# Edge sums by bucket on one core: two of each 16 batches scattered row by row instead of one, and TensorE's first loop placed at the head of a fetch block

## What is computed

```python
edge_aggr = zeros((6250, 128)).at[row].add(edge_features)      # 206,250 rows of 128 fp32
combined  = concat([x, edge_aggr, global], -1) @ W_c + b_c
h   = softplus(combined @ W1 + b1)
h   = softplus(h @ W2 + b2)
out = layernorm(x + h @ W3 + b3)
```

## Time and profile before

| | us |
|---|---|
| median of 3 runs | 1773.76 |
| span of the profiled execution, first to last instruction | 2043.8 |
| of it, to the first scatter of the loop | 68.25 |
| first scatter to the end of the last | 1480.51 |
| from there to the end | 495.04 |
| mean granted TensorE clock in the span | 0.944 |

### The profile page before, as it was taken

How to read it: one execution, slowest core, us unless ns; L and a number is a source line. 1 busy time by engine, 2 the same in 40 slices (tenths; PEclk the granted TensorE clock), 3 DMA queues, 4 the chain that set the end, 5 groups by cost and what they waited for, 6 DMA issues and landing times.

```text
span 2043.8 us, 61008 instructions
## 1 busy us (share of the span) xinstructions
PE 1837.2 (90%) x14853; PEld 1709.6 (84%) x14853; DVE 1309.8 (64%) x3881; ACT 1038.7 (51%) x3479; POOL 1170.9 (57%) x1482
## 2 busy tenths in 40 slices
PE   7888988898898989998998889898988999999986
PEld 4788888888888888887888888788888999999973
DVE  7755555555555555555565555555656998899866
ACT  1443443343444444444443444344446888888886
POOL 1656656656655655665665665565564555555535
PEclk9899988898899999899999898999998999999998
DMA  5488666666656665665565556565657999999942
GB/s 139 156 265 277 198 207 207 202 191 211 207 180 173 174 173 166 175 183 165 172 187 173 172 161 184 163 180 161 186 174 222 299 304 300 296 298 305 304 138 61
DMA packets 166150, 413.19 MB, mean 202 GB/s; under 512 B 28533, under 2 KB 43813, under 8 KB 163896
## 3 DMA queue, kind: packets, MB, share of 16 engines
q1 hardware_dynamic: 103824, 234.69, 38.1%
q0 software_dynamic: 54608, 174.58, 27.5%
q10 hardware_dynamic: 7689, 3.60, 1.0%
HBM read 234.52 MB, written 178.23 MB: 202 GB/s over the span
## 4 chain that ended last, share of the span: by engine, by line
PE 77%; issue 8%; DVE 5%; another core or an unknown queue 3%; POOL 1%; ACT 1%; POOLq 1%; DMA 1%; DVEq 0%; ACTq 0%; SPq 0%
PE ps L1228 51%; PE ps L1300 19%; PE ps L1199 2%; PE ps L1186 2%; DVE arena L803 2%; PE ps L1190 1%; DVE hotc L641 1%; DVE arena L875 1%; PE ps L1335 1%; PE ps L1196 1%; DVE slot_f L660 0%; POOL sums L564 0%; DVE picked L652 0%; POOLq L559 0%
## 5 line engine op out<-in xcount | busy, mean ns | idle before, releaser
L1228 PE MATMUL ps<-arena 128*120 128x129 f32 x9084 | 1229.3, 291 | 98.6 <-issue 87.7
L1228 PEld LDWEIGHTS ps<-arena 128*120 128x120 f32 x9084 | 1141.5, 193 | 130.8 <-issue 117.3
L522 POOL DMA_INDIRECT buckets<-arena,index x757 | 778.8, 1029 | 549.2 <-ACT arena L1013 341.3
L803 DVE TENSOR_SCALAR arena<-slot_no,slot_f 128x360 f32<-128x360 f16 x1514 | 549.1, 415 | 601.3 <-PE ps L1228 332.7
L1013 ACT ACTIVATE arena<-ps 120x387 f32<-120x387 f32 x757 | 372.6, 493 | 851.8 <-PE ps L1228 519.5
L1300 PE MATMUL ps<-mark,members 128*128 128x128 f32 x3648 | 412.7, 276 | 9.0 <-ACT mark L1114 7.1
L1300 PEld LDWEIGHTS ps<-mark,members 128*128 128x128 f32 x3648 | 410.5, 192 | 11.2 <-issue 10.4
L847 DVE TENSOR_SCALAR mark<-node_no,members 128x128 f32<-128x128 f16 x1368 | 360.7, 330 | 55.1 <-DMA members<-buckets 45.9
L564 POOL TENSOR_TENSOR sums<-sums,staged 128x128 f32 x456 | 226.4, 496 | 197.5 <-ACT staged L1102 119.5
L968 ACT ACTIVATE reach<-block_no,arena 128x120 f16<-128x120 f16 x806 | 313.4, 391 | 0.7 <-PE ps L1238 0.7
L1108 ACT ACTIVATE apart<-node_no,members 128x128 f32<-128x128 f16 x456 | 181.0, 397 | 34.3 <-DMA members<-buckets 26.6
(11 more groups left out here) (169 smaller groups left out, 634.6 us busy)
## 6 DMA issues: line engine op xcount, KB each, us to landing
members<-buckets SPq DMA_DIRECT2D x456, 258.0 KB, 3.6
arena<-in_feats SPq DMA_DIRECT2D x201, 516.0 KB
buckets<-arena,index POOLq DMA_INDIRECT x757
xn<-in_x ACTq DMA_DIRECT2D x1, 2800.0 KB
arena<-in_xT SPq DMA_DIRECT2D x11, 250.0 KB, 3.9
out_rows<-xn SPq DMA_DIRECT2D x11, 224.0 KB
buckets<-arena,direct_at POOLq DMA_INDIRECT x98
arena<-in_src SPq DMA_DIRECT2D x1, 805.5 KB
```

The source lines that it names most:

```text
L522: pool.indirect_dma_start(units, bass.IndirectOffsetOnAxis(ap=index[0:SLOTS, s, b:b + 1], axis=0), rows[0:SLOTS, o, :], None).then_inc(sca ...
L803: dve.tensor_scalar(perm[0:TP, b, t, :], slot_no[0:TP, :, :].rearrange("p r b -> p (r b)"), slot_f[0:TP, s, b * TPB + t:b * TPB + t + 1], ...
L1228: mm = pe.matmul(ps[0:SLOTS, MOVED + b, r * ROWF:(r + 1) * ROWF], perm[0:TP, b, t, r * SLOTS:(r + 1) * SLOTS], feat[0:TP, s, b * TPB + t, ...
```

## The change

Batches with k % 8 == 7 are now direct: 100 of 806, two in each body, and list 7 holds nothing else. `direct_at` and `direct_landed` exist twice. The waits between the two kinds on list 7 go. `reached` and `goto` skip direct batches. `firsts` makes 100 entries instead of 50 and runs ahead of the addresses of the head; `rank(0, 1)` comes behind the `rise` matmuls. SyncE waits for landed direct writes at two of the four chunks of a body. TensorE's first loop is told to begin at slot 0 of an instruction fetch block.

```diff
-    DIRECTS = BODIES - 1
+    PERIOD = 8
+    ND = BODY // PERIOD
+    DIRECTS = NBAT // PERIOD
...
         def packed(i, k):
-            return i * (BODY - 1) + (k - min(k // BODY, DIRECTS))
+            return i * (BODY - ND) + (k - k // PERIOD)
         def is_direct(k):
-            return k % BODY == BODY - 1 and k < DIRECTS * BODY
+            return k % PERIOD == PERIOD - 1
+        def ends_direct(s):
+            return (s + 1) * CB % PERIOD == 0
...
             def reload(i, s):
-                if s == XS - 1:
-                    sp.wait_ge(direct_landed, i * (16 * TPB))
+                if ends_direct(s):
+                    sp.wait_ge(direct_landed[s * CB // PERIOD], i * (16 * TPB))
...
-            def scatter_direct(i):
-                pool.wait_ge(direct_ready, i + 1)
-                pool.wait_ge(scattered[STREAMS - 1], i * 16 + 32)
+            def scatter_direct(i, k):
+                d = k // PERIOD % ND
+                pool.wait_ge(direct_ready, directs(i, k) + 1)
...
-            def scatter_body(i):
-                for k in range(BODY - 1):
-                    scatter(i, k)
-                scatter_direct(i)
+            def scatter_body(i, n=BODY):
+                for k in range(n):
+                    if is_direct(k):
+                        scatter_direct(i, k)
+                    else:
+                        scatter(i, k)
...
+            firsts()
+
             dve.tensor_copy(small[0:KS, 5:6], small_i[0:KS, 0:1]).then_inc(base_a, 1)
...
             permutation(0, 0)
             permutation(0, 1)
-            firsts()
...
-            def reached(g, r):
-                wait(act, reach_used, g + 1 - RS)
+            def reached(i, k):
+                if is_direct(k):
+                    return
+                wait(act, reach_used, packed(i, k - RS) + 1)
...
                 act.wait_ge(moved, packed(i, k + 1))
-                if o == STREAMS - 1:
-                    body = i + k // BODY
-                    wait(act, direct_landed, body * (16 * TPB))
-                    wait(act, scattered[o], body * 16 + (32 if k % BODY == BODY - 1 else 16))
-                elif not isinstance(i, int) or turn:
+                if not isinstance(i, int) or turn:
...
             rank(0, 0)
-            rank(0, 1)
             pe.wait_ge(places_made, 1)
             for h, part in enumerate(halves(count_f)):
                 pe.matmul(ps[:, RISE + h, 0:HALF], ...
+            rank(0, 1)
...
-                if not last or k + RS < NBAT:
+                if not is_direct(k + RS) and (not last or k + RS < NBAT):
                     goto(i, k + RS)
...
-            with pe.Fori(1, BODIES - 1) as i:
+            with nc.Fori(1, BODIES - 1, engines=[pe.engine], head_slot={pe.engine: 0}) as i:
```

More of the change, by code:

```diff
@@ L299, in gnn_bucketed_edge_sum_mlp_layernorm @@
         direct_ready = sem("direct_ready")
-        direct_landed = sem("direct_landed")
+        direct_landed = [sem(f"direct_landed{d}") for d in range(ND)]
         scattered = [sem(f"scattered{o}") for o in range(STREAMS)]
@@ L417, in _ @@
             for o in range(STREAMS):
-                sp.wait_ge(scattered[o], (len(range(o, NBAT, STREAMS)) - (DIRECTS if o == STREAMS - 1 else 0)) * 16 + 16)
-            sp.wait_ge(direct_landed, DIRECTS * 16 * TPB)
+                sp.wait_ge(scattered[o], (0 if is_direct(o) else len(range(o, NBAT, STREAMS))) * 16 + 16)
+            for d in range(ND):
+                sp.wait_ge(direct_landed[d], len(range(d, DIRECTS, ND)) * 16 * TPB)
             sp.wait_ge(filled, 16 * FILLS)
@@ L549, in _ @@
                 fill(i, PIECE)
-            with pool.Fori(FILLS, DIRECTS) as i:
+            with pool.Fori(FILLS, BODIES) as i:
                 scatter_body(i)
-            for g in range(DIRECTS * BODY, NBAT):
-                scatter(0, g)
+            scatter_body(BODIES, NBAT - BODIES * BODY)
             pool.wait_ge(window_made, 1)
@@ L657, in slots @@
                 wait(dve, perm_made, packed(i, (s - 1) * CB) * TPB)
-                if s % XS == 1:
-                    wait(dve, direct_ready, i if not isinstance(i, int) else min((c - 1) // XS, DIRECTS))
+                if ends_direct(s - 2):
+                    wait(dve, direct_ready, directs(i, (s - 1) * CB))
                 dve.tensor_reduce(slot_f[0:TP, s % 2, 0:n], picked[0:TP, 0:n, :], AX.X, ALU.add).then_inc(slot_made, 1)
@@ L984, in _ @@
             for g in range(RS):
-                reached(g, g % RS)
+                reached(0, g)
             act.wait_ge(ends_done, 1)
@@ L1025, in _ @@
             for g in range(RS, AHEAD):
-                reached(g, g % RS)
-            indices(0, 0, 0, 0)
+                reached(0, g)
+            indices(0, 0)
             def take(i, k):
@@ L1190, in rank @@
                         pe.matmul(out_[:, :, t, :], ones16[0:TP, 0:TP], hot_[:, :, before, :], start=False, stop=False)
-                if s == XS - 1 and not (isinstance(i, int) and i >= DIRECTS):
-                    body = i
+                if ends_direct(s) and nb == CB:
+                    first = directs(i, s * CB)
                     pe.wait_ge(firsts_made, 2)
                     for part, table in ((first_hi, ident128_16[0:K, :]), (first_lo, ident2_16[0:K, 0, :])):
-                        pe.matmul(out_[:, CB - 1, :, :], part[0:K, bass.ds(body, 1)].to_broadcast([K, TP]),
+                        pe.matmul(out_[:, CB - 1, :, :], part[0:K, bass.ds(first, 1)].to_broadcast([K, TP]),
                                   table.unsqueeze(1).to_broadcast([K, TPB, K]), start=False, stop=False)
@@ L1243, in _ @@
             for k in range(RS):
-                goto(0, k)
+                if not is_direct(k):
+                    goto(0, k)
             def work(i, k):
```

69 lines of the change are left out of this document (37 added, 32 removed).

## The result

The changed kernel takes **1823.01 us** (median of 4 runs, 1821.04 to 1823.57), the kernel before 1774.24 us in the same comparison: ratio 1.027, 95% interval [1.0258, 1.0282]. That is 49 us more where the prediction said 18. The sign and the engine that binds were right, and the time lies inside the range; the size is wrong.

A forecast was written before the change was run, and what follows sets the result against it. GpSimd, nearly level with TensorE before, was to bound the changed loop: head 68.25 + GpSimd 1209 + fills 8 + end 495.04 + 12 around the span = 1792 us; own range 1778 to 1824, whole range down to 1712.

The forecast's parts named there:

- I take 1.31, near the median: Scatter loop: each indirect DMA costs GpSimd 1.31 us (median 1.30, mean 1.33), gap included; 923 make 1209 us.
- End 495.04, taken unchanged: Sums and dense layers behind the scatter loop keep the 495.04 us of the first profile.
- 12 around the span: Outside the profiled span: the metric counts 12 us more, out of 47.5 us left over in the kernel before.
- 35 us of losses: Scatter loop of the kernel before: fill bodies 9, long fills 8, last scatters and first batch 8, small waits 10 us.
- Fills and small losses: Scatter loop: scatters land behind the first four long fills, some 2 us missing each, 8 us in all; bounds 0 and 20.
- TensorE at 1163 before and 1094 after: Scatter loop: TensorE's work priced from undisturbed trace rows, 1.43 us a packed batch and 0.37 a rank; 69 us less.
- Loads, cost 0: Chunk reloads waiting for direct writes to land: covered, 0 us; upper bound twice the 11.0 us of load waits.
- Loop head 0: Placing TensorE's first loop at a fetch block's start costs or gives 0; at most part of 87.7 us.
- head hidden: Before the loop: `firsts` and one more rank ahead of the first moves are hidden behind GpSimd's gap writes; otherwise +1.3 us.
- Packets 0: DMA queues in the scatter loop: 516-byte rows replacing 1548-byte blocks add little to some 76% load, 0 us.
- Rival A: GpSimd's DMAs are cheaper unprofiled, for instance because part of the 0.30 us gap is the profiler's: 1722 us, chance 0.33.
- D: Rival: GpSimd's DMA price rises to 1.33 us as VectorE grows denser: 1811 us; shares the forecast's 0.50 chance.

The follow-up runs named there:

- the second trace of before: The kernel before, unchanged, run and profiled once more: ratio 1.0003, profiled span 1772.4 us instead of 2043.8.

## Why the prediction was wrong in size

Point by point, against the profiled execution of after (1819.1 us of span, 1821.04 us in all, 2 us under the median):

| term | taken | measured | off by |
|---|---|---|---|
| head | 68.25 | 68.31 | 0.1 |
| 923 DMAs on GpSimd | 1209 (1.31 each) | 1225.8 (1.328 each) | 16.8 |
| fills, idle | 8 | 15.4 | 7.4 |
| end | 495.04 | 509.6 | 14.6 |
| around the span | 12 | 1.9 | -10.1 |
| sum | 1792.3 | 1821.0 | 28.7 |

- **What binds** was right, and the step that found it: GpSimd's 0.30 us belongs to its price, and the 51 DMAs more fall on an engine that had 26 us to spare, so that TensorE's relief can't be used. "Two engines are nearly level" holds too, with TensorE ahead where a body has no fill.
- **The step that failed first is GpSimd's price.** "I take 1.31, near the median" threw the long instructions away as few, some of them beside the creeping. They are no outliers: every one over 1.04 us in the kernel after started while VectorE was inside a `hot` or a `permutation`, and the second trace of before is free of creeping and has a *higher* mean, 1.050 us and the gap, 1.354. The prediction's own mean bound, 1.33, was the right value. A sum over a saturated engine takes the mean. Whether an instruction is long for a reason that will go is a separate question, and it was not asked.
- **"End 495.04, taken unchanged" failed second.** For the kernel before it was right within its spread (495.0 to 498.2 us in the traces of its code, with a loop placed or not), but it took code that the diff doesn't touch as costing the same. The place of GpSimd's sums loop is worth 5.7 us of the difference, shown in one profile; the cause of the 4.4 us behind the sums stays open.
- **"12 around the span"** is 1.9 us. This and the 35 us of losses were fitted to 47.5 us that the clean price left over. GpSimd, not the metric, held part of it: 26.3 us idle beside 1180.6 us of its own work in a loop of 1206.9 us.
- **Fills and small losses**: 15.4 us of idle time in place of 8, inside the bounds of 0 to 20.
- **TensorE at 1163 before and 1094 after** can be tested only where TensorE binds. Without half the direct writes its turn was 22.1 and 23.3 us: the clean prices give 14 x 1.43 + 4 x 0.37 + 2 x 0.10 = 21.7, and 15 x 1.43 + 4 x 0.37 + 0.13 = 23.06. Right within 2%.
- **Loads, cost 0**: the cost is right, the view of the queue was not. ScalarE waits 344.3 us for them, far over "twice the 11.0 us". The time is covered since GpSimd lies in arrears anyway.
- **Loop head 0, head hidden**: right. **Packets 0**: no run tests it by itself, and GpSimd's count and price leave 15.4 us of the loop for everything else (the batches are 806, not 807). The head grew by 1.0 us against the second trace of before, under the bound of 1.3, but it varies by up to 2 us between these runs (66.9 to 68.8).
- **What would show it**: 706 and 200 rows, the 0.30 us gap and the 8472 moves came as said; GpSimd's busy time was 944.9 us for 951. Two steps came out differently. TensorE waits for ScalarE's `reach`, 77.7 us, and not for its rows, and the span shrank by 225 us and not 20 to 50, since the creeping was not in the second profile at all.
- **Rival A** falls: the timed run and the profile agree to 2 us, so the profiler adds nothing to GpSimd's 0.30 us that counts. **D** gave 1811 from the right price, 1.33, and VectorE is the right engine, but the change didn't make it denser (busy 72% of the loop before, 67% after), GpSimd's busy time fell from 1.050 to 1.024 us with it, and with 381 us of VectorE's work apart the price is the same. D rests on the Trainium skill (SBUF — State Buffer, Who interferes with whom), by which GpSimd's descriptor writes stand still during VectorE's two-port modes. The traces agree that a descriptor instruction waits out the VectorE instruction it starts in (1171 ns for 994 with 300 to 360 ns left); in which mode `hot` and `permutation` run they don't say.
- The Trainium skill's advice on large descriptors (Perfetto Trace Analysis, What "DMA-bound" means) agrees with the runs: GpSimd's price doesn't grow with the bytes, with 1033 ns for 120 blocks of 1548 bytes and 996 ns for 128 rows of 516 bytes. Whether it hangs on the DMAs or on their blocks no run tells, since all had 120 to 128.

## What to carry to other kernels

When two engines share a loop, add up for each the mean busy time and the fixed gap behind every instruction, not the busy share and not the median: an engine at 67% "busy" can be the one that never rests. An instruction that is sometimes long isn't an outlier until its cause is known; look what the other engines are in when the long ones start. Moving work from one to the other pays only as far as the slack of the receiver, and here GpSimd had 26 us where the change asked for 68. And if a profiled span doesn't match the timed runs, profile again before any share of it is used.

## What was not expected

- One profiled execution can be 270 us (15%) longer than all timed ones, with TensorE creeping at a granted clock of 0.94 in the loop; the same kernel profiled again had 1772.4 us and 0.99.
- Code that isn't touched can take longer when code ahead of it changes length: 11.4 us (0.6%) here, of which 5.7 us are traced to a loop's place. For TensorE's first loop, TensorE's sums loop and GpSimd's last scatter loop the place meant nothing; for GpSimd's sums loop it was worth 5.7 us over 56 turns, some 0.1 us a turn.
- Long waits can stand on an engine that isn't on the path: 344 us of waits for loads could be taken away whole, and the loop didn't become shorter.
- GpSimd's price per indirect DMA differs between kernels (1.015 to 1.050 us busy) with a constant gap of 0.304 us. Neither the amount of VectorE's work nor the place of GpSimd's loop explains it; by the traces it is how often, and how early, a descriptor instruction starts inside VectorE's `hot` or `permutation`.
